# Flamingo-style two-layer block on one core: the contexts' beta moved into the latents and a constant row, normalisation moved to GpSimd, and a new order of VectorE's and ScalarE's late work

## The reference, cut to what matters

```python
x = x + tanh(g_xattn[0]) * xattn_A(ctx, layernorm(x), mask, ...)   # 8 heads of 64
x = x + tanh(g_ffn[0])   * moe(layernorm(x), ...)                  # 8 experts, top 2
x = x + tanh(g_xattn[1]) * xattn_B(ctx, layernorm(x), mask, ...)   # 16 heads of 64
x = x + tanh(g_ffn[1])   * conv_ffn(layernorm(x), ...)             # quantised, depthwise conv
# both attentions, in essence:
xn  = layernorm(ctx) * gamma + beta           # 375 rows
lat = layernorm(latents) * gamma_l + beta_l   # 112 rows; latents are layernorm(x)
q = lat @ Wq;  k, v = concat([xn, lat]) @ Wkv # layer A: lat is gated inside keys and values
out = softmax(mask(q k / 8)) v @ Wout         # over 487 keys
```

## Time and profile before

| | us |
|---|---|
| median of 3 runs | 1533.12 (1521.33 to 1535.54) |
| profiled execution, its own time | 1539.58 |
| span of its instructions | 1537.8 |
| PE busy | 1267.6 (82%) |
| POOL busy | 1111.4 (72%) |
| DVE busy | 1067.4 (69%) |
| ACT busy | 979.5 (64%) |

### The profile page before, as it was taken

How to read it: one execution, slowest core, us unless ns; L and a number is a source line. 1 busy time by engine, 2 the same in 40 slices (tenths; PEclk the granted TensorE clock), 3 DMA queues, 4 the chain that set the end, 5 groups by cost and what they waited for, 6 DMA issues and landing times.

```text
span 1537.8 us, 44950 instructions
## 1 busy us (share of the span) xinstructions
PE 1267.6 (82%) x16822; PEld 983.6 (64%) x16822; DVE 1067.4 (69%) x2846; ACT 979.5 (64%) x2319; POOL 1111.4 (72%) x1359
## 2 busy tenths in 40 slices
PE   0777787679869979868999999899999999998842
PEld 0555565558657866646878878566676676766642
DVE  4669888976556656665666666777778777878744
ACT  2669787455546666645656565777777777777731
POOL 4768888686557765467677867798888888887754
PEclk9979999879989989989999999999999999999965
DMA  9599998495999954358999998445545545444320
GB/s 316 129 190 237 252 231 180 81 223 154 246 201 249 232 125 92 72 111 209 243 247 254 254 245 197 84 95 105 105 80 96 101 103 98 95 96 90 79 38 6
DMA packets 438329, 239.95 MB, mean 156 GB/s; under 512 B 388848, under 2 KB 420320, under 8 KB 429024
## 3 DMA queue, kind: packets, MB, share of 16 engines
q1 hardware_dynamic: 408216, 178.51, 55.1%
q10 hardware_dynamic: 26824, 51.22, 10.7%
q0 software_dynamic: 3072, 7.34, 1.8%
HBM read 107.78 MB, written 35.50 MB: 93 GB/s over the span
## 4 chain that ended last, share of the span: by engine, by line
PE 35%; ACT 15%; DVE 12%; POOL 12%; DMA 10%; issue 9%; DVEq 3%; SPq 3%; ACTq 2%; POOLq 0%
PE bank_ring L1088 7%; PE bank_ring L1126 6%; PE bank_ring L1074 5%; DVE scores L1339 5%; DMA expert_up<-experts_up 4%; ACT scores L849 4%; PE bank_out L1107 4%; ACT probs L856 3%; PE bank_x L1187 3%; POOL probs L654 3%; DMA probs_turned<-probs 3%; ACT values L876 3%; PE bank_x L1140 3%; PE bank_scores L1048 2%; DMA context<-in_ctx 2%
## 5 line engine op out<-in xcount | busy, mean ns | idle before, releaser
L654 POOL TENSOR_TENSOR probs<-scores,probs 112x487 f16<-112x487 f32 x384 | 426.0, 1126 | 237.0 <-ACT probs L856 232.5
L849 ACT ACTIVATE scores<-scores,score_min 112x487 f32<-112x487 f32 x384 | 265.9, 694 | 131.0 <-DVE score_min L1339 129.9
L1356 DVE SCALAR_TENSOR_TENSOR values<-bank_ring,values 128x512 f16<-128x512 f32 x192 | 132.3, 689 | 213.9 <-ACT values L876 213.3
L1339 DVE CUSTOM_DVE_ANT_0 scores<-bank_scores,mask 112x487 f32<-112x487 f32 x384 | 238.0, 656 | 2.7 <-PE bank_scores L1048 2.7
L856 ACT ACTIVATE probs<-scores 112x487 f16<-112x487 f32 x384 | 214.0, 604 | 27.1 <-DMA probs_turned<-probs 11.7
L1088 PE MATMUL bank_ring<-weights,kv_B 128*128 128x128 f16 x3072 | 197.5, 222 | 1.2 <-DVE keys L1351 1.2
L1088 PEld LDWEIGHTS bank_ring<-weights,kv_B 128*128 128x128 f16 x3072 | 186.5, 100 | 10.4 <-DVE keys L1351 2.0
L876 ACT ACTIVATE values<-bank_ring 128x512 f16<-128x512 f32 x192 | 113.0, 588 | 123.7 <-PE bank_out L1107 119.6
L1107 PE MATMUL bank_out<-values,probs_turned 128*128 128x64 f16 x4608 | 172.7, 195 | 20.5 <-issue 11.4
L1074 PE MATMUL bank_ring<-kv_B,weights 128*128 128x488 f16 x768 | 181.0, 372 | 0.0
L1107 PEld LDWEIGHTS bank_out<-values,probs_turned 128*128 128x128 f16 x4608 | 160.8, 100 | 24.6 <-issue 16.8
(11 more groups left out here) (230 smaller groups left out, 2426.8 us busy)
## 6 DMA issues: line engine op xcount, KB each, us to landing
expert_up<-experts_up SPq DMA_DIRECT2D x43, 1024.0 KB, 5.4
expert_down<-experts_down SPq DMA_DIRECT2D x43, 512.0 KB, 6.6
raw_weights<-in_weights ACTq DMA_DIRECT2D x8, 1536.0 KB, 11.3
experts_up<-expert_up ACTq DMA_DIRECT2D x8, 1024.0 KB, 4.6
raw_weights<-in_weights ACTq DMA_DIRECT2D x6, 1024.0 KB, 7.9
probs_turned<-probs SPq DMA_TRANSPOSE x384
context_turned_B<-kv_B ACTq DMA_DIRECT2D x16, 375.0 KB, 8.1
kv_B<-context_turned_B ACTq DMA_DIRECT2D x16, 375.0 KB, 3.8
```

Of the source, the lines that this page charges most:

```text
L654: pool.tensor_tensor(PR[:, u % 4, 1, 0:KEYS], S[:, u % 4, 0:KEYS], PR[:, u % 4, 0, 0:KEYS], ALU.subtract).then_inc(probs_split, 1)
L849: act_e.activation(S[:, u % 4, 0:KEYS], S[:, u % 4, 0:KEYS], ACT.Exp, bias=rmin[:, u % 4:u % 4 + 1], scale=-1.0, accum_out=rsum[:, g % 2, ...
L1339: dve.tensor_tensor_reduce(out=S[:, u % 4, 0:KEYS], in0=bS[u % 2][0:TOK, 0:KEYS], in1=mask[:, m, 0:KEYS], scale=1.0, scalar=3.0e38, op0=AL ...
L1356: dve.scalar_tensor_tensor(vN[:, j % 2, 1].rearrange("p t d -> p (t d)"), bank("v", j)[:], 1 / WSCALE, vN[:, j % 2, 0].rearrange("p t d -> ...
```

## The change

1. **Beta.** The contexts carry gamma times the normalised rows only. The latents' part in keys and values gets its own beta less the contexts' (`V_GATED`, `V_LAT_B`). The constant row that is missing from the output is computed once for each layer on PE (`v_shift`: beta times the values' weights, 24 and 48 one-column products; `o_shift`: times the output weights, 12 and 24 products of 256 columns) and added to each sequence's x by POOL (`shift_row`).
2. **Contexts.** POOL normalises (`apply_context`). ACT writes both layers' high halves straight from the bank of the transpose, DVE both low halves from the same bank; `rawT` and `split_context` are gone. Layer A has three slots instead of two (`KV_SLOTS`). ACT's reading of a transpose comes at the end of the same step, no more in the next one, and so does its wait for the spill before last.
3. **Latents.** ACT writes the affine latents in fp32 from the bank (four pieces, for layer B too, where it was two), POOL casts and subtracts. `p_lat` is transposed one step later, at the end of 4n-5, but split one step sooner, in 4n-4, and layer B's queries read `latents_Q` too.
4. **Order on DVE.** Where no expert tile starts in the next step, the low half of the values of step j is made after the masks of step j + 1. The drains of late tasks come at the end of their own step, before the next masks; only those of `p_turn` stay behind the masks, and the row maximum's four scalars go there (`second_scale`), now after `norm_out`. `m_turn` moves from early to late for most sequences.
5. **Zeroing.** Twelve stores of up to 4 slots leave on ACT's queue in steps 27 to 32 instead of five on SP's at the start; DVE clears 4 slots of `xr` and both `kv` tiles whole.

```diff
+ZERO_STEP, ZERO_EACH = 27, 2
+ZERO_PIECES = [(b, at, min(ZERO_ROWS, t - at)) for b, t in enumerate(TILES) for at in range(0, t, ZERO_ROWS)]
+SHIFT_STEPS = (0, 61)
+KV_SLOTS = (3, 2)
+def row_step(layer, n):
+    return start_b(n) + 3 if layer else max(4 * n + 1, 3)
@@ late(j)
-        if j == 4 * n - 6:
+        if j == 4 * n + 10 and slack(n):
+            tasks.append(("m_turn", n))
+        if j == 4 * n - 5:
             tasks.append(("p_lat", n))
+PROMPT = ("p_turn", "p_lat", "b_lat", "m_turn")
 def halves_in_step(j):
-    return is_pair(j)
+    return is_pair(j) and micro(j + 1)[0] is not None
@@ sync
             sp.wait_ge(zeros_set, 1)
-            for b in range(2):
...
-                    sp.dma_start(rows[:, at:at + n], xr[:].rearrange("p s c -> p (s c)")[:, 0:n])\
-                        .then_inc(rows_zeroed, 16)
@@ gpsimd
-            def split_context(n, kb, layer):
...
             def split_latents(layer, n):
...
+                for i, dst in enumerate(places):
+                    last = pool.tensor_copy(dst[:, :, 0], affl[:, i])
                 after(last)
+                for i, dst in enumerate(places):
+                    last = pool.tensor_tensor(dst[:, :, 1], affl[:, i], dst[:, :, 0], ALU.subtract)
...
+            def apply_context(n):
+                pool.wait_ge(rstd_ready["P"], n + 1)
+                for t in range(CT):
+                    last = pool.tensor_scalar(ctxb[0:CP, n % 2, t, :], ctxb[0:CP, n % 2, t, :],
+                                              mv["P"][0:CP, t, 0:1], rs["P"][0:CP, t:t + 1], ALU.subtract, ALU.mult)
+                last.then_inc(ctx_normed, 1)
+            def shift_row(layer, n):
...
+                pool.tensor_tensor(X[:, n], X[:, n], oshift[:], ALU.add).then_inc(row_shifted, 1)
@@ scalar
+                for piece in ZERO_PIECES[max(ZERO_EACH * (j - ZERO_STEP), 0):max(ZERO_EACH * (j - ZERO_STEP + 1), 0)]:
+                    zero_rows(*piece)
                 if name == "p_turn":
                     kb = task[2]
-                    act_e.wait_ge(x1_drained, X1_AT[task])
+                    act_e.wait_ge(x1_filled, X1_AT[task])
+                    if n >= KV_SLOTS[0]:
+                        act_e.wait_ge(v_ready, 4 * (n - 2))
                     if n >= 2:
                         act_e.wait_ge(spilled[n % 2], 16 * (n // 2))
+                    for layer in range(2):
+                        c = 8 * layer + V_GAMMA + kb
+                        last = act_e.activation(kv(layer, n)[:, kb, 0, TOK:KEYS], bX1[:, 0:CTX],
+                                                ACT.Identity, scale=vec[:, c:c + 1])
+                elif name in ("p_lat", "b_lat"):
...
+                    for i, c in enumerate((8 * layer + V_GLAT, V_LAT_B if layer else V_GATED)):
+                        for kb in range(KB):
...
+                            last = act_e.activation(affl[:, i, kb], bX1[:, TOK * kb:TOK * kb + TOK], ACT.Identity,
+                                                    scale=scale, bias=shift)
+                for t in late(j):
+                    if t[0] in PROMPT:
+                        part(t)
@@ vector
+                    dve.wait_ge(ctx_hi, 2 * n + kb + 1)
+                    for layer in range(2):
+                        c = 8 * layer + V_GAMMA + kb
+                        last = dve.scalar_tensor_tensor(kv(layer, n)[:, kb, 1, TOK:KEYS], bX1[:, 0:CTX],
+                                                        vec[:, c:c + 1], kv(layer, n)[:, kb, 0, TOK:KEYS],
+                                                        ALU.mult, ALU.subtract)
@@ vector, the loop over steps
-                for t in late(j - 1):
-                    part(t)
...
                 if is_pair(j - 1) and not halves_in_step(j - 1):
                     split_v(j - 1)
+                for t in late(j - 1):
+                    if t[0] == "p_turn":
+                        part(t)
+                    elif t[0] == "f_max":
+                        second_scale()
...
                 if halves_in_step(j):
                     split_v(j)
+                for t in late(j):
+                    if t[0] != "p_turn":
+                        part(t)
```

295 lines of the change are left out of this document (150 added, 145 removed).

## The result

The changed kernel took 1525.9 us (median of 20 runs, 1514.8 to 1545.7) against 1537.4 us for the kernel before on the same chips (20 runs): a ratio of 0.9938 with a 95% interval of 0.9912 to 0.9964. The forecast was a gain of 4.5%; the gain is 0.6%. Its profiled execution spans 1522.9 us, that of before 1537.8.

What follows compares the result with a forecast made beforehand. It took PE as layer B's busiest engine (464.6 of 516 us), no engine owning layer A; 11 + 22 + 30 + 3 + 6 + 1 - 6 + 2 = 69 us off 1539.58 gave 1465 us on the median's scale, range 1445 to 1480.

Steps and rivals of the forecast that it cites:

- Layer A, the step that failed: Layer A: PE's waits for mask and copies go, a third is given back; gain 22 us, ends 5 and 45.
- The ports rival: GpSimd's three normalisations and the splits they meet stretch each other through shared ports; 1484 us, chance 0.07.
- The DMA rival: DMA bounds layer A, which then gives 4 instead of 22 us; 1483 us, chance 0.13.
- Lead-in: Start of the kernel: context 3 no longer waits behind 5.5 MB of zero stores; gain 11 us, ends 4 and 14.09.
- What is late next: Lead-in: POOL's normalisations, ACT's and DVE's transpose readings, latents and mask come next; mask seen at 32.8 us before.
- Layer B: Low half of values leaves the ring, late products move; 2.6 to 2.7 us a period, 30 us, ends 8 and 45.
- Zero stores: Stores moved to ACT's queue at steps 27 to 32 cost 0 us there; ends 0 and 6.
- Batch 0: First expert batch: waits for expert weights, which nothing here touches; gain 3 us, ends -3 and 8.
- POOL or ACT bounding layer B: Layer B: POOL or ACT becomes the bound, a period gives 0.9 instead of 2.7 us; 1485 us, chance 0.12.
- ACT behind the spill: ACT waits for the spill of two sequences before to land, holding masks and PE; 1540 us or more, chance 0.04.
- Prices: Instruction costs assumed: constant row 6 us on PE; halves read from PSUM 0.47 us on ACT, 0.54 on DVE.

Runs made afterwards that it cites:

- the order alone: Kernel before with only VectorE's order changed (values' low half behind the next masks, late products drained at the end of their step): 0.9787, 1507.5 us; again 0.9788, 1502.4 us.
- zero_first: Changed kernel with its 12 zero stores issued at the front of SyncE's queue again: 0.9925 of the kernel before, 1524.4 us.
- norm_first: Changed kernel with contexts normalised by VectorE and expert splits right behind the masks: 0.9873 of the kernel before, 1516.9 us.
- splits_first: Changed kernel with VectorE's expert splits right behind the masks, ahead of the queries' and values' low halves: 0.9891 of the kernel before, 1520.9 us.
- splits_last: Changed kernel with VectorE's expert splits behind the keys' low half, at the end of the step: 0.9946 of the kernel before, 1523.0 us.
- dve_norm: Changed kernel with VectorE normalising the contexts again, at the steps used before the change: 0.9835 of the kernel before, 1514.2 us.
- row_small: Changed kernel with GpSimd adding one column of the constant row instead of 256 in layer B: 0.9867 of the kernel before, 1519.5 us.
- spill_early: Changed kernel with each context's spill issued one step earlier: 0.9910 of the kernel before, 1522.1 us.
- best2: Changed kernel with three edits: contexts normalised by VectorE, expert splits behind the keys' low half, latents copied by VectorE; 0.9927 of the kernel before, 1523.2 us.
- its half: Kernel before with only the late products drained at the end of their own step, values' low half left in its step: 1.0044, 1542.0 us.

## Why the prediction was wrong

The sign was right, the size was not: 69 us forecast, 11 measured by the medians and 15 by the two profiles, and the time lies outside the range. Two profiles of the changed kernel and two of the order alone divide the change in two. The order alone: lead-in +1.5, steps 0 to 7 -1.2, steps 8 to 26 +6.4, steps 27 to 37 -1.2, batch 0 -7.6, bridge -6.3, batch 1 +2.6, layer B -28.6, together -34 us. Everything else on top of it (context, latents, constant row, zero stores, ScalarE's order): -7.3, +10.9, +4.5, +5.7, -3.7, +2.1, -3.0, +10.2, together +19 us. What I valued most is a loss. There is one profile of the kernel before, and two of one kernel differ by up to 7 us in a stage (batch 0 of the order alone: 207.4 and 200.5), so the small terms are rough.

- **Layer A, the step that failed.** "I give a third back and take 22 us", from the waits of the earlier trace rows, "which I took from waits and not from a bound". The waits went, as said. But a wait that goes shortens a stage only if nothing else fills its place, and the sum had no term for that beyond a third. In place of -22 there stood +23.5: 7.2 in steps 0 to 7 with their stalled step, 10.9 in steps 8 to 26, 4.7 at the moved zero stores (zero_first), 0.7 behind them. Only some 4 of it are the order's (two profiles); the rest came with everything else. Of the 10.9, taking the stretch away saved about 9 (norm_first and splits_first, in the steps that were not stalled). But the order alone costs 6.4 in these steps almost without a stretch, and splits_last took 6 less than the changed kernel with all of it. The causes overlap, and their shares stay open.
- **The ports rival had the mechanism and the wrong partner.** It priced the normalisations. They took 1.39 us in steps 8 to 26 for the 0.66 I took, but hardly by being stretched: the median of all 48 is 1.22 us, which is also what those with DVE idle took. The price by columns was wrong. GpSimd had the time, and taking them away left steps 8 to 26 at 149.7 us. The pair that costs is the expert splits beside the probs subtraction, which the kernel before had too, only not at the same time. I read the one 3.470 of the earlier trace rows as a rare event of an affine, and did not ask which two instructions the removed affines had kept apart. The Trainium skill ("SBUF — State Buffer", section on the two separate sides) has the lock for DVE operations with two SBUF inputs; the splits are such, and the trace agrees in the waits by turns (1.21, 1.57, 1.60 us). The trace shows besides that `x_normed_M`, a `TENSOR_SCALAR` with one tile and two scalars from SBUF, is stretched as well: 807 ns on average in steps 8 to 26, against 405 to 410 where GpSimd was idle.
- **The DMA rival** said that layer A would give 4 instead of 22 us. Its sign was that the waits for transposes would grow; they did (17.6 us, the largest of PE in this stage, against 8.0 before), and the share of the stage is 0.93. Layer A came out worse than its price (-4), so it explains a part at most: the stall is one of transfers, in the changed kernel a stretch of 10 us (86 to 96 us) at 21 to 81 GB/s, where the stage moves 195 on average. That the mean share bounds the other steps is not shown: norm_first's other steps fell by 0.5 us each at a share of 0.96.
- **Lead-in: mis-sized.** -5.1 for -11. The third context no longer waits, but the chain now runs through GpSimd's normalisations, 3.66 and 6.44 us. Here one was stretched: 2.62 us beside DVE's weight splits, for the usual 1.22. With DVE's normalisations the lead-in was 9.7 us shorter than before (dve_norm). "What is late next" had listed them and priced them at nothing.
- **Layer B: the order's part was right, the context's part had the wrong sign.** Forecast 2.6 to 2.7 us a period; the order alone gave 2.5 and 2.6. I had let 0.4 of it come from the latents, which the order alone does not touch; in truth everything else took 1.0 back. I priced ScalarE's four latent pieces at 0.26 us each by the queries' row; they took 0.446, so that PE's wait is 1.42 us, as long as before the change (1.37 in the earlier trace rows). The row's addition costs 0.3 a period. Why the other 0.7 is lost is open: copying the latents by DVE made the period longer, not shorter.
- **Zero stores** at steps 27 to 32: "0 us; ends 0 and 6". It was 4 to 6 against zero_first, near the upper end (in row_small, with the stores still there, these steps took 51.0 us, 2 more than in zero_first).
- **Batch 0**: -10.5 for -3. The order alone has -4.2 and -11.1 in its two profiles, so most of it need not be the context's doing; the spread is as large as the term.
- **POOL or ACT bounding layer B, and ACT behind the spill.** POOL stands at 40.9 us a period (40.4 forecast), and no wait for it over 0.2 us shows on PE in layer B. ScalarE never waited for a spill to land, but for the issuing of one, 18 us at one place.
- **Prices.** The constant row took PE 6.4 us in all (0.74, 1.52, 1.34 and 2.78) where I had 6. The halves read from PSUM took 0.57 us on ScalarE for my 0.47, and 0.60 on DVE for my 0.54.

**Open** stays what makes packets of one load take up to 12 us in one step of layer A, and whether such steps explain how widely a kernel's runs spread (1515 to 1546 us for the changed one). Of the 13 profiles of kernels with the changed contexts, 8 show it: six at step 6 (one of them, splits_first, also at step 15), norm_first at step 15 and spill_early spread over steps 6 and 7; best2 has a milder one at steps 15 and 16 (15 packets of 12,288 bytes up to 5.7 us, step 16 11.5 us). The four of the kernel before, of the order alone and of its half have no stalled step, which is too little to call them free of it. Single parts of everything else on top of the order alone were not tried, so which of them costs what there is not shown.

## What to carry to other kernels

Work taken off an engine that is not the bound moves what stands behind it to an earlier time; before calling it a gain, look for pairs of instructions on VectorE and GpSimd that now meet, and price them by the stretched duration in the trace (here up to 1.60 for 0.68 us). An instruction's time can't be taken from its columns where its operations differ: 1.22 us for GpSimd's normalisation, where 0.66 was the guess. Where two engines wait for one another in a ring, moving a single 0.69 us instruction out of it was worth 27 to 34 us of layer B, while everything but the order made the kernel 19 us longer. Waits of one engine for a bank that many products share can't be summed up as a gain: two cures that removed such a wait of 1.4 us made the period 0.7 and 2.3 us longer.

## What the runs showed of the hardware

- A DVE `SCALAR_TENSOR_TENSOR` of 512 columns with both inputs in SBUF took 0.68 us alone and up to 1.60 us beside GpSimd's `TENSOR_TENSOR` of 487 columns, which took 1.56 instead of 1.11. Each ended a little less than its own time behind the other's end (0.54 and 0.98 us), as if it had waited for it. One with a PSUM input (375 columns, line 1641) took 0.60 us throughout.
- GpSimd's `TENSOR_SCALAR` that subtracts and then multiplies took 1.22 us (median) for 256 columns in f32; the one that multiplies and then adds took 0.675 (median) for 375 columns in the kernel before.

```profile
L650 POOL TENSOR_SCALAR context<-context,mean_var_P,rstd_P x48: 1208/1223/2619, 16.2 to 503.3; 125x256 f32<-125x256 f32 x48
```

- ScalarE's reading of PSUM with a scale from a tile took 0.57 us for 375 columns and, with a bias and f32 output, 0.446 for 112, where a plain copy of 112 takes 0.26.
- Issuing one DMA of 375 KB held ScalarE for 18.0 us, behind 3.4 MB issued in the 5 us before it; in the other profiles with a stall at step 6 it took 8.8 to 16.9 us, in kernels with the changed contexts and no stall there 4.9 to 5.4. From 82.0 to 104.2 us 127 GB/s were moved. PE was busy for 7.5 of these 22.2 us and stood idle from 84.7 to 88.3 us; its granted clock was 1.00 up to 84 us and 0.50, the lower of the two levels (1.2 GHz), from 86 us on, and then 0.94 on average from 104.2 to 258.6 us.
- In the changed kernel the 18 packets of 12,288 bytes that began between 82 and 86 us took 7.5 us on average; the 31 that began between 94 and 98 us took 0.47. In row_small 54 began between 82 and 86 us and took 0.46.
